# Eight tiles of probabilities, one mixing for each batch, and the FFN's low halves on VectorE, in a new order of operations

## The chip, the core and the metric

The kernel runs on one core of a Trainium2 chip. The metric is the device time of one execution in microseconds, the median of several runs. The engines are TensorE (PE), VectorE (DVE), ScalarE (ACT) and GpSimd (POOL); SP only issues DMAs. Each takes its instructions in the order of its own queue and waits at semaphores.

## The reference

64 batches of 128 tokens with 256 features pass through four residual blocks, each on the layer norm of x:

```
x = x + attention0(norm(x), ctx, mask)      # 16 heads of 16, biases, mask int32
x = x + ffn0(norm(x))                       # ternary W1, W2: relu(x W1' + b1) W2 + b2
x = x + attention1(norm(x), ctx, valid_len) # 16 heads of 16, no biases
x = x + ffn1(norm(x))                       # base + adapter of one of 8 experts
```

In an attention, scores are softmax(q k^T / 4) over 128 keys, and the output is that times v, times w_o. In ffn0, h = relu(...) has 1024 features. In ffn1 each batch takes the expert whose reconstruction relu(x Wd1 + bd1) Wd2 + bd2 is nearest to x, summed over the batch, and adds relu(x Wa_down + ba_down) Wa_up + ba_up of that expert.

## The kernel before

A pass handles a pair of batches (PB = 2, T = 256 tokens); there are NP = 32 pairs. The whole is a software pipeline written out by hand in slots. Each engine has one loop over the slots t, and `for p in at(t, 48)` runs an operation for the pair p whose slot 48 is t. BODY = 16 slots start a new pair, so operations of up to six pairs stand interleaved on each engine. The order within a slot and the slot numbers fix each queue's order. Waits are on counting semaphores: `signal.done(engine, p, n)` makes an engine wait for the n-th event of pair p.

Attention of layer l, for a pair: 8 steps j, each with four heads of one batch. `scores(l, p, j)` writes 128x512 scores into the one bank S. `maximum` on VectorE takes the row maxima from it. After four steps `split_max` splits the 16 maxima of a batch into fp16 halves and transposes them, and `maxima` on SP moves them into rows of qs by four DMAs. `scores_t` then computes the transposed scores less the maxima in the bank X, `exps` on ScalarE writes their exponentials into the tile pT, and for layer 0 `apply_mask` on GpSimd multiplies them by the mask. pT has 4 buffers of 128x512. `mix(l, p, u)` multiplies two buffers by the values in 8 matmuls (16 instructions, as each fp32 matmul is two) of 128 rows and 32 columns, which write the four column strips of the bank V; two mixings fill V for one batch. `turn_out` on VectorE transposes V, `scale_out` divides by the sums and transposes again into attT, and `output` multiplies by w_o. `add_att` adds to x.

q and k are kept as two fp16 halves: `high` on ScalarE copies the projection's bank as fp16, `low` on VectorE subtracts that. `spill` writes both to DRAM and `stack` reads them back with heads rearranged into qs and ks; both are issued by SP.

The FFN of layer 0: `ffn_up(p, j)`, four of them, write 128x512 into a bank. `relus` on ScalarE writes relu into work[j % 2] in fp32, `h_highs` on ScalarE rounds that to fp16 (hhl, part 0), and `h_lows` on GpSimd subtracts the rounded from the exact value (hhl, part 1). `ffn_down` for each of the two batches multiplies both parts by w2q.

ffn1: `hidden` and `reconstruct` (four, two experts each; 64-row matmuls), `differences` on VectorE, `squares` on ScalarE, `losses`, `choose`, a `gather` of the adapter by SP, `down` and `up`.

Layer norms: `statistics` on VectorE, `rstd_of` and `normalise` on GpSimd, `turn` on TensorE. `mask_parts`, `mask_bias` and `add_bias` are GpSimd's as well. `rstd_of(0, p)` also waits for `any_of` (VectorE), which reduces the mask to a column.

The other results of TensorE share five PSUM banks, D0 to D4; the table BANKS says which. A matmul that writes a bank waits for the consumer of the bank's last content.

Of the kernel before, what the change touches and what calls it, by code (L numbers as in the profile page):

```python
# [33 lines left out]
UNITS = 2 * PB  # L34
# [13 lines left out]
def pair16(value):  # L48
# [17 lines left out]
    ("cnt", "rec5", "v1", "hd0", "q0"),  # L66
    ("v0", "q1", "T2", "F1_1", "T0", "hd1", "T3"),
    ("O0", "F1_2", "rec1", "loss", "rec7", "up"),
    ("O1", "k0", "rec6", "rec3", "F2", "down", "rec0"),
    ("rec2", "F1_0", "T1", "k1", "F1_3", "rec4"),  # L70
# [27 lines left out]
def build(nc, x, lens, mask, mask_t, wq0, bq0, wk0, bk0, wv0, bv0, wo0, bo0, w1t, b1, w2t, b2,  # L98
          wq1, wk1, wv1, wo1, w_base, wd1, bd1, wd2, bd2, adapters, ctx_in, out):
    with ExitStack() as ctx:  # L100
# [76 lines left out]
        pT = sb("pT", [P, 4, 512], F32)  # L177
# [41 lines left out]
        mix_ready = [signal(f"mix_ready{l}", UNITS) for l in range(2)]  # L219
# [101 lines left out]
        def _(sp):  # L321
# [84 lines left out]
            for t in range(FIRST, END):  # L406
                for p in at(t, 48):
                    maxima(1, p, 1)
                for p in at(t, -14):
                    load(p)  # L410
                for p in at(t, 34):
                    stack(1, 1, p)
                    spill(1, 0, p)
                for p in at(t, 4):
                    maxima(0, p, 0)
                for p in at(t, 36):
                    stack(1, 0, p)
                for p in at(t, 71):
                    gather(p)
                for p in at(t, -7):  # L420
                    spill(0, 1, p)
                for p in at(t, 10):
                    maxima(0, p, 1)
                for p in at(t, -6):
                    stack(0, 1, p)
                for p in at(t, -5):
                    spill(0, 0, p)
                for p in at(t, 44):
                    maxima(1, p, 0)
                for p in at(t, -4):  # L430
                    stack(0, 0, p)
                for p in at(t, 76):
                    store(p)
                for p in at(t, 29):
                    spill(1, 1, p)
# [9 lines left out]
        def _(pool):  # L445
# [73 lines left out]
            def apply_mask(p, j):  # L519
                exp_done[0].done(pool, p, j)  # L520
                keep_ready.done(pool, p)
                blk = pT[:, j % 4].rearrange("p (a t) -> p a t", a=4)
# [3 lines left out]
            def h_lows(p, j):  # L526
                h_high.done(pool, p, j)
                nc.gpsimd.tensor_tensor(hhl[:, 1, 2 * j:2 * j + 2], work[:, j % 2], hhl[:, 0, 2 * j:2 * j + 2],  # L528
                                        ALU.subtract).then_inc(h_low.sem, 1)

            for t in range(FIRST, END):
                for p in at(t, 16):
                    normalise(1, p, 0)
                for p in at(t, 19):
                    normalise(1, p, 1)
                for p in at(t, -11):
                    mask_parts(p)
                    rstd_of(0, p)
                for p in at(t, -10):
                    normalise(0, p, 0)  # L540
                    normalise(0, p, 1)
                for p in at(t, 6):
                    apply_mask(p, 0)
                for p in at(t, 7):
                    apply_mask(p, 1)
                for p in at(t, 23):
                    h_lows(p, 0)
                for p in at(t, -8):
                    mask_bias(p)
                for p in at(t, 8):  # L550
                    apply_mask(p, 2)
                for p in at(t, 24):
                    h_lows(p, 1)
                for p in at(t, 9):
                    apply_mask(p, 3)
                for p in at(t, 26):
                    add_bias(1, p)
                for p in at(t, -6):
                    add_bias(0, p)
                for p in at(t, 26):  # L560
                    h_lows(p, 2)
                    h_lows(p, 3)
                for p in at(t, 10):
                    apply_mask(p, 4)
                for p in at(t, 58):
                    rstd_of(3, p)
                for p in at(t, 59):
                    normalise(3, p, 0)
                    normalise(3, p, 1)
                for p in at(t, 11):  # L570
                    apply_mask(p, 5)
                for p in at(t, 12):
                    apply_mask(p, 6)
                for p in at(t, 13):
# [15 lines left out]
        def _(act):  # L590
# [32 lines left out]
            def exps(l, p, j):  # L623
                st_ready[l].done(act, p, j)
                if j >= 4:
                    mix_ready[l].done(act, p, (j - 4) // 2)
                elif l:
                    mix_ready[0].done(act, min(p + 2, NP - 1), 2 + j // 2)
                    mix_ready[1].done(act, p - 1, 2 + j // 2)
                else:  # L630
                    mix_ready[1].done(act, p - 3, 2 + j // 2)
                    mix_ready[0].done(act, p - 1, 2 + j // 2)
                nc.scalar.activation(pT[:, j % 4], X[:], ACT.Exp, scale=SCALE).then_inc(exp_done[l].sem, 1)  # L633
# [54 lines left out]
            for t in range(FIRST, END):  # L688
                for p in at(t, 48):
                    exps(1, p, 2)  # L690
                for p in at(t, 64):
                    squares(p, 1)
                for p in at(t, 49):
                    exps(1, p, 3)
                for p in at(t, 66):
                    squares(p, 2)
                for p in at(t, 50):
                    exps(1, p, 4)
                for p in at(t, 34):
                    copy_xT(2, p)  # L700
                for p in at(t, 67):
                    squares(p, 3)
                for p in at(t, 51):
                    exps(1, p, 5)
                for p in at(t, 35):
                    high(1, 0, p)
                for p in at(t, 67):
                    squares(p, 4)
                for p in at(t, 52):
                    exps(1, p, 6)  # L710
                for p in at(t, 20):
                    copy_xT(1, p)
                for p in at(t, 68):
                    squares(p, 5)
# [3 lines left out]
                for p in at(t, 69):  # L718
                    squares(p, 7)
                for p in at(t, 6):  # L720
# [3 lines left out]
                for p in at(t, -9):  # L724
                    high(0, 1, p)
# [742 lines left out]
```

## Time and profile before

| | |
|---|---|
| median of 3 runs | 1717.36 us |
| lowest and highest | 1717.09 and 1728.58 us |
| profiled execution, own time | 1727.22 us |
| its span in the trace | 1725.2 us |
| PE busy | 1584.5 us (92%) |
| DVE busy | 1316.8 us (76%) |
| ACT busy | 891.8 us (52%) |
| POOL busy | 1104.2 us (64%) |

The span runs from the first to the last instruction of one profiled execution. Busy shares are means over the span, which has a ramp at either end in which few pairs are in flight. A busy TensorE is not one at its peak, since ends of matmuls are modelled; the starts are measured, so costs are read as the distance between starts.

### The profile page before, as it was taken

Reading aid. Unit: us, or ns where it says so; the run is one execution under the profiler, and the core shown is the slowest. Engines: PE = TensorE matmul, PEld = TensorE weight load, DVE = VectorE, ACT = ScalarE, POOL = GpSimd, SP = SyncE. Lnnn points to the kernel's source line nnn. Section 1 sums busy time; section 2 is a strip of 40 time slices with the busy share of each in tenths; the row PEclk is TensorE's granted clock in tenths of the full one; section 3 lists DMA queues with packets and bytes.
Section 4 is the critical chain, followed back from the end, with each engine's and each line's share of the span. In section 5 each row is a group of like instructions: output and inputs, shape, how many; then the busy total and the mean of one; then the engine's idle time right before and its main releaser. Section 6 shows DMA issues by size and latency. Waiting matters only on the chain.

```text
span 1725.2 us, 44058 instructions
## 1 busy us (share of the span) xinstructions
PE 1584.5 (92%) x15136; PEld 1279.1 (74%) x15136; DVE 1316.8 (76%) x5086; ACT 891.8 (52%) x2465; POOL 1104.2 (64%) x1198
## 2 busy tenths in 40 slices
PE   2578999999999999999999999999999999999776
PEld 1356777778878887778887877788788877877554
DVE  6446788888887888888887888888788888886542
ACT  0134455655555556555555556555555565555432
POOL 4467776666676776666667766666677766655200
PEclk9789999999999999999999999999999999999976
DMA  7445555555555454555555545555555555552300
GB/s 187 81 74 92 87 88 92 96 103 97 97 95 108 83 96 96 103 97 94 97 103 94 94 90 98 101 95 99 97 106 82 97 97 102 97 77 54 57 18 26
DMA packets 286213, 157.24 MB, mean 91 GB/s; under 512 B 38820, under 2 KB 281640, under 8 KB 285992
## 3 DMA queue, kind: packets, MB, share of 16 engines
q1 hardware_dynamic: 285992, 154.44, 49.6%
q8 instruction: 121, 1.98, 0.6%
q14 instruction: 100, 0.82, 0.2%
HBM read 111.36 MB, written 41.96 MB: 89 GB/s over the span
## 4 chain that ended last, share of the span: by engine, by line
PE 47%; DVE 38%; issue 7%; DMA 3%; POOL 2%; ACT 1%; SPq 1%; DVEq 0%; ACTq 0%; POOLq 0%
DVE dump L863 11%; PE psD L1239 7%; PE psD L1228 7%; DVE dif L929 6%; PE psD L1207 4%; PE psD L1153 4%; PE psD L1273 4%; PE psS L1168 3%; PE psD L1142 3%; PE psV L1195 3%; PE psX L1180 3%; DVE atok L894 3%; PE psD L1249 3%; DVE otok L886 2%; DVE m L872 2%
## 5 line engine op out<-in xcount | busy, mean ns | idle before, releaser
L633 ACT ACTIVATE pT<-psX 128x512 f32<-128x512 f32 x512 | 305.9, 597 | 351.7 <-PE psX L1180 351.6
L523 POOL TENSOR_TENSOR pT<-pT,keep 128x512 f32<-128x512 f32 x256 | 323.1, 1268 | 108.2 <-ACT pT L633 105.6
L508 POOL TENSOR_SCALAR xn<-xr,mv,rstd 128x256 f32<-128x256 f32 x256 | 311.5, 1224 | 13.7
L855 DVE TENSOR_REDUCE mx<-psS 128x4 f32<-128x512 f32 x256 | 175.7, 686 | 170.8 <-PE psS L1168 168.4
L482 POOL TENSOR_SCALAR veps<-mv 128x2 f32<-128x2 f32 x128 | 29.5, 230 | 392.3 <-DVE mv L808 389.6
L929 DVE SCALAR_TENSOR_TENSOR dif<-psD,bd2s,xT 128x256 f32<-128x256 f32 x512 | 216.8, 472 | 63.6 <-PE psD L1249 63.5
L863 DVE CUSTOM_DVE_ANT_0 dump<-psS,bias 128x128 bf16<-128x128 f32 x1024 | 232.5, 282 | 30.8 <-PE psS L1168 30.7
L1168 PE MATMUL psS<-ks,qs 65*128 65x128 f16 x2048 | 202.6, 221 | 49.2 <-DVE mx L863 22.6
L677 ACT ACTIVATE dif<-dif 128x256 f32<-128x256 f32 x512 | 207.4, 412 | 25.8 <-DVE dif L929 24.7
L1180 PE MATMUL psX<-qs,ks 67*128 67x128 f16 x2048 | 200.4, 220 | 15.5 <-ACT pT L633 8.7
L1168 PEld LDWEIGHTS psS<-ks,qs 65*128 65x128 f16 x2048 | 141.6, 98 | 97.8 <-issue 34.0
L1180 PEld LDWEIGHTS psX<-qs,ks 67*128 67x128 f16 x2048 | 141.6, 98 | 55.6 <-issue 18.6
L1195 PE MATMUL psV<-pT,v 128*32 128x128 f32 x4096 | 165.9, 280 | 8.0 <-POOL pT L523 4.3
L528 POOL TENSOR_TENSOR hhl<-work,hhl 128x512 f16<-128x512 f32 x128 | 151.5, 1193 | 11.9 <-ACT hhl L663 11.9
L1207 PE MATMUL psD<-wo,attT 128*128 128x256 f32 x512 | 132.1, 403 | 19.3 <-DVE attT L898 19.2
L1249 PE MATMUL psD<-hd,wd2s 64*128 64x256 f32 x1024 | 146.3, 405 | 2.0 <-DVE dif L929 2.0
L1195 PEld LDWEIGHTS psV<-pT,v 128*32 128x32 f32 x4096 | 96.8, 109 | 61.4 <-issue 39.3
L1220 PE MATMUL psD<-xs,w1q 128*128 128x256 f16 x1024 | 134.0, 274 | 1.4 <-DVE xs L911 0.8
L1142 PE MATMUL psD<-xT,wq 128*128 128x256 f32 x512 | 132.0, 394 | 1.5 <-DVE keep L822 1.5
L1153 PE MATMUL psD<-wv,ctxT 128*128 128x256 f32 x512 | 130.5, 399 | 0.0
L606 ACT ACTIVATE xT<-psD 128x512 f32<-128x512 f32 x96 | 57.1, 595 | 137.4 <-PE psD L1113 137.4
L1239 PE MATMUL psD<-xT,wd1s 128*128 128x256 f32 x512 | 126.0, 390 | 0.7 <-ACT xT L606 0.7
(103 smaller groups left out, 3125.3 us busy)
## 6 DMA issues: line engine op xcount, KB each, us to landing
scr<-packed SPq DMA_DIRECT2D x128, 256.0 KB, 2.3
ks<-scr SPq DMA_DIRECT2D x256, 128.0 KB, 4.5
qs<-scr SPq DMA_DIRECT2D x256, 128.0 KB, 4.4
adapter<-in_adapters SPq DMA_DIRECT2D x64, 192.5 KB, 2.5
xr<-in_x SPq DMA_DIRECT2D x32, 256.0 KB, 2.8
ctxT<-in_ctx SPq DMA_DIRECT2D x32, 256.0 KB, 2.8
qs<-mrows SPq DMA_DIRECT2D x512, 2.0 KB
out_y<-xr SPq DMA_DIRECT2D x32, 256.0 KB, 4.9
```

What stands on the lines that cost most here:

```text
L508: nc.gpsimd.tensor_scalar(xn[:, XN[s], b], xr[:, p % NX, b], mv[:, s, b, 0:1], rstd[:, s, b:b + 1], ALU.subtract, ALU.mult).then_inc(norme ...
L523: nc.gpsimd.tensor_tensor(blk, blk, keep[:, p % 2, j // 4].unsqueeze(1).to_broadcast([P, 4, P]), ALU.mult).then_inc(masked.sem, 1)
L633: nc.scalar.activation(pT[:, j % 4], X[:], ACT.Exp, scale=SCALE).then_inc(exp_done[l].sem, 1)
L677: nc.scalar.activation(blk, blk, ACT.Square, accum_out=acc[:, e, b:b + 1]).then_inc(squared.sem, 1)
L863: ins = nc.vector.tensor_tensor_reduce(out=dump[:, a], in0=S[:, a * P:a * P + P], in1=bias0[:, p % 2, b], scale=1.0, scalar=-3e38, op0=ALU ...
L929: nc.vector.scalar_tensor_tensor(out=dif[:, e % 4, k], in0=bank[f"rec{e}"][:, k * T:k * T + T], scalar=bd2s[:, e, k:k + 1], in1=xT3[:, p % ...
L1153: ins = nc.tensor.matmul(dst[:, b * D:b * D + D], ctxT[:, p % NC, k * T + b * P:k * T + b * P + P], wv[l][:, k], start=(k == 0), stop=(k = ...
L1168: ins = nc.tensor.matmul(S[:, a * P:a * P + P], qs[0:MASK_ROW + 1, r, h, t0:t0 + P], ks[0:MASK_ROW + 1, r, h, t0:t0 + P], start=True, stop ...
L1180: ins = nc.tensor.matmul(X[:, a * P:a * P + P], ks[0:ROWS, r, h, t0:t0 + P], qs[0:ROWS, r, h, t0:t0 + P], start=True, stop=True)
L1195: ins = nc.tensor.matmul(V[32 * a:32 * a + 32, (2 * half + s) * P:(2 * half + s) * P + P], v2[l][:, b, half * UH + 2 * a + s], pT[:, (2 * ...
L1207: ins = nc.tensor.matmul(dst[:, b * D:b * D + D], attT[:, l, b, k], wo[l][:, k], start=(k == 0), stop=(k == KD - 1))
L1239: ins = nc.tensor.matmul(dst[:, m * T:m * T + T], wd1s[:, k, e0:e0 + 2].rearrange("p e r -> p (e r)"), xT3[:, p % 2, k], start=(k == 0), s ...
```

## The change

pT gets 8 buffers, one for each step j. A mixing is now one of 16 matmuls (32 instructions) for a batch, `mix(l, p, b)`: it waits for the fourth exponential (or mask) of its batch. `exps` waits for the mixing that last read its buffer, of the other layer. `h_lows` moves from GpSimd to VectorE (the same function, there on nc.gpsimd). BANKS is dealt anew, and nearly every operation of every engine gets another slot or another place in its slot. Nothing of what is computed changes.

```
-        pT = sb("pT", [P, 4, 512], F32)
+        pT = sb("pT", [P, QUADS, 512], F32)
...
             def exps(l, p, j):
                 st_ready[l].done(act, p, j)
-                if j >= 4:
-                    mix_ready[l].done(act, p, (j - 4) // 2)
-                elif l:
-                    mix_ready[0].done(act, min(p + 2, NP - 1), 2 + j // 2)
-                    mix_ready[1].done(act, p - 1, 2 + j // 2)
+                if l:
+                    mix_ready[0].done(act, min(p + 2, NP - 1), j // 4)
                 else:
-                    mix_ready[1].done(act, p - 3, 2 + j // 2)
-                    mix_ready[0].done(act, p - 1, 2 + j // 2)
-                nc.scalar.activation(pT[:, j % 4], X[:], ACT.Exp, scale=SCALE)
+                    mix_ready[1].done(act, p - 3, j // 4)
+                nc.scalar.activation(pT[:, j], X[:], ACT.Exp, scale=SCALE)
...
+            def h_lows(p, j):
+                h_high.done(dve, p, j)
+                nc.vector.tensor_tensor(hhl[:, 1, 2 * j:2 * j + 2], work[:, j % 2], hhl[:, 0, 2 * j:2 * j + 2],
+                                        ALU.subtract).then_inc(h_low.sem, 1)
...
-            def mix(l, p, u):
-                b, half = u // 2, u % 2
-                if half == 0:
-                    claim("V", turned[l], p, b)
-                if u == 0:
+            def mix(l, p, b):
+                claim("V", turned[l], p, b)
+                if b == 0:
...
-                (exp_done[1] if l else masked).done(pe, p, 2 * u + 1)
-                for s in range(2):
+                (exp_done[1] if l else masked).done(pe, p, 4 * b + 3)
+                for n in range(4):
                     for a in range(4):
-                        ins = nc.tensor.matmul(V[32 * a:32 * a + 32, (2 * half + s) * P:(2 * half + s) * P + P],
-                                               v2[l][:, b, half * UH + 2 * a + s], pT[:, (2 * u + s) % 4, a * P:a * P + P],
+                        ins = nc.tensor.matmul(V[32 * a:32 * a + 32, n * P:n * P + P],
+                                               v2[l][:, b, n // 2 * UH + 2 * a + n % 2], pT[:, 4 * b + n, a * P:a * P + P],
```

The new order, by slot modulo 16 (`op@slot`), where the prediction speaks of it:

```
TensorE  0 values(1)@48, scores(0,0)@0, scores_t(1,2), reconstruct 1
         6 scores_t(0,0), scores(0,6), ffn_up 0@22, losses@70, mix(1,1)@54
         8 count@-8, keys(1)@24, scores_t(0,2), scores(1,0)@40, ffn_up 2@24
         9 ffn_up 3@25, scores_t(0,3), scores(1,1), turn(0)@-7, output(1)@57
        10 scores(1,2), down@74, scores_t(0,4), queries(0)@-6, mix(0,0)@10
        11 scores(1,3), scores_t(0,5), up@75
        12 ffn_down 0, scores_t(0,6), turn(3), scores(1,4)
        13 ffn_down 1, scores(1,5), scores_t(0,7), hidden 0
        14 scores_t(1,0), scores(1,6)
        15 hidden 1, scores(1,7), mix(0,1)@15, reconstruct 0@63, scores_t(1,1)
VectorE  0 differences 0, 1, scale_out(0,1)@16, maximum(0,0)@0, differences 2
         6 any_of@-10 (was -12), maximum(0,6), low(0,1), choose, values0, scale_out(1,0)
         7 maximum(0,7), h_lows 0@23
         8 split_max(0,1), maximum(1,0), turn_out(1,1), scale_out(1,1)@56
         9 maximum(1,1), h_lows 1, add_att(1)
        10 any_rows, maximum(1,2), h_lows 2, statistics(3)
        11 h_lows 3, low(0,0), maximum(1,3)
        12 turn_out(0,0), low(1,1)@28 (was @24, slot 8), add_up, split_max(1,0)@44, maximum(1,4)
        15 maximum(1,7), turn_out(0,1)@15, split_max(1,1)@47
GpSimd   4 mask_parts@-12, rstd_of(0)@-12
         5 mask_bias, apply_mask 0, normalise(0,0)
         6 apply_mask 1, normalise(0,1)   7 add_bias(0), apply_mask 2   8 apply_mask 3
SP      10 spill(0,0)@-6, maxima(1,0)@42 (was @44)   11 spill(1,1)@27, stack(0,0)@-5
        12 store, maxima(1,1)@44
```

Before, the four mixings of a pair and layer stood in slots 0, 2, 4, 6 (layer 1) and 9, 11, 13, 15 (layer 0), reconstruct 0 before mix(0,3), and differences 0 and turn_out(0,1) at the end of slot 15.

## Rows read from the trace of the kernel before

**Rows 1.** Stretches: busy us (x instructions) of each engine, TensorE's clock, DMA share, GB/s.
```profile
903.00:923.30 20.30, 19.41 (x199) 15.53 (x195) 19.92 (x93) 15.03 (x44) 15.87 (x19) 1.00 0.39 80
...
923.30:946.10 22.80, 22.67 (x206) 19.02 (x207) 14.85 (x38) 8.78 (x21) 18.36 (x19) 1.00 0.55 85
```

**Rows 2.** The chain of waits, in order of time: start us, us, what.
```profile
897.40 0.29 DVE dump L863
...
923.43 1.97 PE psD L1207 x8
```

**Rows 3.** TensorE in order of time: start, us, line, tiles, shapes, count, [idle before].
```profile
916.00 0.40 PE L1168 MATMUL psS<-ks,qs 65*128 65x128 f16 x4 [0.40 <-DVE mx L863]
...
972.38 1.97 PE L1207 MATMUL psD<-wo,attT 128*128 128x256 f32 x8 [0.55 <-DVE attT L898]
...
976.64 1.05 PE L1264 MATMUL psD<-xT,adapter 128*128 128x128 f32 x8
...
977.62 0.65 PE L1195 MATMUL psV<-pT,v 128*32 128x128 f32 x16
...
981.31 0.39 PE L1168 MATMUL psS<-ks,qs 65*128 65x128 f16 x4
...
985.93 0.39 PE L1180 MATMUL psX<-qs,ks 67*128 67x128 f16 x4
986.25 0.64 PE L1195 MATMUL psV<-pT,v 128*32 128x128 f32 x16
...
991.39 1.13 PE L1249 MATMUL psD<-hd,wd2s 64*128 64x256 f32 x8
992.45 0.65 PE L1195 MATMUL psV<-pT,v 128*32 128x128 f32 x16
993.03 1.99 PE L1153 MATMUL psD<-wv,ctxT 128*128 128x256 f32 x8
```

**Rows 4.** VectorE in order of time, same columns.
```profile
905.55 1.66 DVE L929 SCALAR_TENSOR_TENSOR dif<-psD,bd2s,xT 128x256 f32<-128x256 f32 x4
...
907.67 0.65 DVE L837 TENSOR_TENSOR packed<-psD,packed 128x512 f16<-128x512 f32 x1
...
913.27 0.75 DVE L845 TENSOR_TENSOR v<-psD,bvb 128x256 f32<-128x256 f32 x2
...
921.11 0.68 DVE L837 TENSOR_TENSOR packed<-psD,packed 128x512 f16<-128x512 f32 x1
...
921.99 0.82 DVE L894 TENSOR_TENSOR atok<-otok,rden 128x256 f32<-128x256 f32 x1
...
944.42 0.77 DVE L886 STREAM_TRANSPOSE otok<-psV 128x256 f32<-128x256 f32 x2
```

**Rows 5.** VectorE and GpSimd in order of time, around two forms of contact.
```profile
905.37 2.43 POOL L508 TENSOR_SCALAR xn<-xr,mv,rstd 128x256 f32<-128x256 f32 x2
...
907.32 0.18 DVE L872 SCALAR_TENSOR_TENSOR m<-mx,m 128x16 f16<-128x16 f32 x1
...
910.72 0.41 DVE L814 TENSOR_REDUCE allc<-mqf 128x2 f32<-128x256 f32 x1
...
911.88 2.43 POOL L508 TENSOR_SCALAR xn<-xr,mv,rstd 128x256 f32<-128x256 f32 x2
...
918.40 1.16 POOL L528 TENSOR_TENSOR hhl<-work,hhl 128x512 f16<-128x512 f32 x1
...
918.51 1.08 DVE L872 SCALAR_TENSOR_TENSOR m<-mx,m 128x16 f16<-128x16 f32 x1
...
919.66 1.52 POOL L476 TENSOR_SCALAR bias<-mqf,allc 128x128 f32<-128x128 f32 x2
...
921.26 1.27 POOL L523 TENSOR_TENSOR pT<-pT,keep 128x512 f32<-128x512 f32 x1
```

**Rows 6.** SP's queue in order of time, and DMA issues of 900 to 949 (us to landing).
```profile
921.10 2.69 SPq L377 DMA_DIRECT2D qs<-mrows  x4
...
qs<-scr SPq DMA_DIRECT2D x8, 128.0 KB, 4.4
```

More of the change, by code:

```diff
@@ L433, in _ @@
                     store(p)
-                for p in at(t, 29):
-                    spill(1, 1, p)
+                for p in at(t, 44):
+                    maxima(1, p, 1)
                 if LATE_SLOT <= t < LATE_SLOT + len(LATE):
@@ L521, in apply_mask @@
                 keep_ready.done(pool, p)
-                blk = pT[:, j % 4].rearrange("p (a t) -> p a t", a=4)
+                blk = pT[:, j].rearrange("p (a t) -> p a t", a=4)
                 nc.gpsimd.tensor_tensor(blk, blk, keep[:, p % 2, j // 4].unsqueeze(1).to_broadcast([P, 4, P]),
                                         ALU.mult).then_inc(masked.sem, 1)
[L526 to L529, printed above, removed]
             for t in range(FIRST, END):
@@ L737, in _ @@
                     h_highs(p, 1)
+                for p in at(t, 9):
+                    exps(0, p, 3)
                 for p in at(t, -7):
@@ L741, in _ @@
                     h_highs(p, 2)
-                for p in at(t, 9):
-                    exps(0, p, 3)
                 for p in at(t, 26):
@@ L751, in _ @@
                     a_relus(p)
+                for p in at(t, 27):
+                    high(1, 1, p)
                 for p in at(t, -5):
@@ L973, in _ @@
                 for p in at(t, 64):
+                    differences(p, 0)
                     differences(p, 1)
+                for p in at(t, 16):
+                    scale_out(0, p, 1)
                 for p in at(t, 0):
                     maximum(0, p, 0)
-                for p in at(t, 16):
-                    scale_out(0, p, 1)
-                for p in at(t, 65):
+                for p in at(t, 64):
                     differences(p, 2)
@@ L990, in _ @@
                     statistics(1, p)
-                for p in at(t, 50):
+                for p in at(t, 67):
+                    differences(p, 4)
+                for p in at(t, 51):
                     turn_out(1, p, 0)
@@ L995, in _ @@
                 for p in at(t, 67):
-                    differences(p, 4)
                     differences(p, 5)
-                for p in at(t, 4):
+                for p in at(t, 3):
                     split_max(0, p, 0)
@@ L1327, in _ @@
                     scores_t(1, p, 7)
-                for p in at(t, -11):
-                    count(p)
                 for p in at(t, 5):
@@ L1345, in _ @@
                     scores(0, p, 7)
+                for p in at(t, 23):
+                    ffn_up(p, 1)
+                for p in at(t, -8):
+                    count(p)
                 for p in at(t, 24):
-                    ffn_up(p, 1)
                     keys(1, p)
@@ L1401, in _ @@
                     scores_t(1, p, 0)
-                for p in at(t, 47):
-                    scores(1, p, 7)
+                    scores(1, p, 6)
                 for p in at(t, 63):
```

292 lines of the change are left out of this document (141 added, 151 removed).

## The prediction

> **What bounds the kernel now.** I read the stretches first. In the middle of the run TensorE is granted its full clock (1.00, that is 2.4 GHz) and is busy 19.4 of 20.3 us and 22.7 of 22.8 us [rows 1]. It looks like a kernel bound by TensorE, but the same rows show VectorE busy 19.9 of 20.3 us in the first stretch and 14.9 of 22.8 us in the second. So I read the chain of waits next. It has two legs: it runs on VectorE from the first maximum of layer 0 (897.40) to the last transpose before output(1), and output(1) on TensorE starts when that lands (923.43) [rows 2]. From there it runs on TensorE alone to the next pair's first maximum. Output(1) starts again at 972.38 [rows 3], so a pair costs 48.95 us: 26.0 on VectorE, 22.9 on TensorE, 31 times over. The TensorE timeline shows what the VectorE leg costs TensorE: 0.55 us idle before output(1) and 0.40 before a scores block [rows 3]. Measured from start to start these are about 0.7 and 0.57 us. TensorE's blocks alone fill some 47.7 us of the 48.95.
>
> So two sums must be made: what TensorE's own work becomes, and what the loop through both engines becomes. The larger one is the period.
>
> **TensorE's own work.** A mixing of 16 instructions takes 0.58 us (992.45 to 993.03) [rows 3]. Eight full-array fp32 instructions of 128 columns (down) take 0.98 us including 0.09 before the mixing behind them, thus 0.11 each [rows 3]. Four column strips run side by side, so 0.58 is 4 x 0.11 plus 0.14 for leaving the mode. Entering it costs 0.09: scores before a mixing hold TensorE 0.32 us (985.93 to 986.25) where 0.23 is usual. A mixing of 32 is then 8 x 0.11 + 0.14 = 1.01 us, for 1.15 before. Four of these a pair save 0.56. The new order has 6 entries into a tiled mode instead of 8 (mixings stand next to reconstruct or losses), 0.19 more. Fewer fp32 blocks stand behind an f16 block, some 0.1 to 0.2. TensorE's own work falls from 47.7 to 46.8 us. The lower end is that 32 instructions run at the pace of the down block throughout: 46.8. The other end is that 64 instructions in a row are issued no faster than before: 47.3.
>
> **VectorE's leg.** VectorE gets four subtractions of 128x512. The nearest row is the low half of a key, 0.68 us from PSUM, 0.60 from start to start [rows 4]. Sources in SBUF may be anything from 0.55 to 0.68; I take 0.60. Only h_lows 0 stands in the leg that bounds; 1 to 3 stand behind output(1), where VectorE was idle 8 us a pair [rows 1]. In exchange low(1,1) leaves the leg (-0.60). At the front, turn_out(0,1) (944.42, 0.7 from start to start), a split_max and two differences (2.12 together, 905.55 to 907.67) [rows 4] now stand ahead of maximum(0,0). Before, they ran beside values(1). The leg now starts when mixing (0,1) is done, not at the first maximum. Of the old 26.0 us, 1.3 were blocked time (below). So the new leg unblocked is 26.0 - 1.3 + 2.8 + 0.6 - 0.6 = 27.5 us.
>
> **TensorE's leg of the loop** is from output(1) to the end of mixing (0,1). Before, output(1) to the last mixing's start took 20.07 (972.38 to 992.45) [rows 3]. Out of it go two mixings (1.15), reconstruct 0 (1.06, 991.39 to 992.45), which now follows, one scores block with it (0.23) and one entry (0.09). In comes one mixing of 1.01. That is 18.55; plus 1.01 for mixing (0,1) itself and 0.2 until VectorE sees it: 19.75. The loop is 27.5 + 19.75 = 47.25 us before any blocking, already above TensorE's 46.8.
>
> **What VectorE waits for on GpSimd.** The same 16-element instruction (L872) takes 0.18 us while GpSimd normalises, a tensor_scalar (907.32 in 905.37 to 907.80), and 1.08 us while it runs a tensor_tensor (918.51, until 919.56) [rows 5]. The multiply of scale_out(1,1) took 0.82 for 0.42 behind a mask multiply that began at 921.26 [rows 4, 5]. That is the 1.3 us. The multiply ends 0.28 after GpSimd's operation; it starts 0.14 before the end of it. So I take it that VectorE operations with two SBUF sources wait for a running tensor_tensor of GpSimd. h_lows is one. The change removes four tensor_tensor from GpSimd, but GpSimd stays busy without a gap from mask 0 to mask 3: GpSimd now stands in rstd_of(0) until VectorE's any_of, which moved two slots later, and then has a backlog.
>
> Both queues start from any_of, so their phase can be worked out. GpSimd: 0.8 us of small operations until it starts its next large one (from 910.72 + 0.41 to 911.88) [rows 5]; then mask_bias, 1.6 (919.66 to 921.26); then mask 0, normalise, mask 1, normalise and add_bias, each 1.22 from start to start, as the two normalises of 2.43 [rows 5]. So mask 1 runs from 4.8 to 6.1 us after any_of, and mask 2 starts at 8.5. VectorE: before, the eleven operations from values0 to the multiply of scale_out(1,1) took 8.72 (913.27 to 921.99) [rows 4]. The new order has the same ones between any_of and that multiply, with h_lows 0 for low(1,1), so 7.73 unblocked. The multiply of scale_out(1,0) meets mask 0's end (0.2). h_lows 0 comes at 5.2, in mask 1: it waits 0.8. The multiply of scale_out(1,1) then comes at 8.7, 0.2 to 0.3 after mask 2 began: it waits 0.95. Together 1.95 us for 1.3 before. The loop is 49.2. The bounds are no blocking at all (47.25) and a full operation before each of five candidates, some 5 us (52).
>
> The page SBUF - State Buffer of the Trainium skill (Who interferes with whom) says that a VectorE instruction with two SBUF inputs contends with a GpSimd instruction that reads SBUF. It speaks against this change. The trace agrees for tensor_tensor (1.08 for 0.18 us), not for normalise, which reads SBUF too; the fourth rival is what the whole rule would give.
>
> **The other queues.** ScalarE keeps its work, in new slots with idle time before most of it. exps no longer wait for half mixings: nothing waited there that the chain shows, so zero. If ScalarE were late, mask 2 would be, and the block at 8.7 would go. The SP queue: maxima(1,0), whose row maxima are ready only two slots later, now holds spill(1,1) and stack(0,0) behind it; see the slow rival.
>
> **From period to time.** The ramps (223 us) keep their shape; TensorE's savings of 0.9 us a pair count there for some four pairs, -3 or -4 us. Likeliest: 31 x (49.2 - 48.95) = +8, less 4: +4. The profiled execution took 1727.2 us (span 1725.2) and would take about 1731. The median of the three runs is 1717.4, so I put 1720 there. Under 1% (17 us) I call no difference.
>
> **Rivals.**
> The phase falls well (faster): if VectorE is 0.3 us earlier, or mask 2 later, the multiply of scale_out(1,1) starts at once. The period is 48.2: -23 - 4, 1690. For it: the margin is 0.2 to 0.3 on a sum of twenty durations. Against: h_lows 0 is locked to mask 1's end, so what follows has a fixed phase. Chance 0.25.
> TensorE is all that counts (much faster): hardly any blocking, period 47.2: -54 - 4, 1660. This needs GpSimd idle where the profile shows backlog. Chance 0.09.
> SP's queue becomes late (slower): from the end of up, VectorE does add_up and split_max(1,0) (1.2), SP issues maxima (2.7), the spill (0.4) and four stacks (2.7 at most, like maxima), which land 4.4 later [rows 6]: 11.5 us. TensorE has 13.3 from up to the next scores(0,0) (981.31 to 993.03 and 1.8 for values, less 0.2). The reserve is 1.8 plus 0.5 that the first maximum waits anyway. From there on each us is a us a pair. Two blocks of 1.1 at split_max's two operations, or landings 2 us longer under the load of the other transfers, use it up. With those and a third block in the first leg the period is 50.2: +39 - 4, 1752. Chance 0.21.
> GpSimd's normalise blocks the subtraction as well (slower): then split_max(0,1) behind h_lows 0 waits for the rest of a normalise, 1.1, and the multiply before it for another 0.6. The period is 50.9: +60 - 4, 1773. The row at 907.32 is against it. Chance 0.03.
> The mixing of 32 takes twice the time of 16 (that part doing nothing): 0.28 on the loop, 1729, inside the likeliest case.
>
> **Chances.** Likeliest 0.42 (1703 to 1734), fast phase 0.25, floor 0.09, the two slow ones 0.24. Faster by over 1% 0.34, within 1% 0.41, slower 0.25. The range reaches to the fast phase and into the slow case: 1678 to 1754.
>
> **What would show it.** Mixing from first to next start 1.01 us; VectorE's share near 88 to 90%; GpSimd's share down by about 5 us a pair; h_lows on VectorE longer than 0.68 us in the profile for the first of four; output(1) still released by attT, with TensorE idle about 2 us there; the chain still VectorE then TensorE. I am wrong if output(1) is released without idle time, if the subtraction is blocked by nothing, or if scores(0,0) waits for qs<-scr.

## The result, and the profile after

The median went from 1718.43 to 1734.69 us (8 runs each, 1716.68 to 1728.58 and 1731.21 to 1741.07): a ratio of 1.0072, 95% interval 1.0050 to 1.0094. The ratio is not the quotient of those two medians (1.0095): the kernel before scatters by nearly as much as the change costs, five of its eight runs from 1716.68 to 1719.50 and three from 1724.63 to 1728.58, and its median on the chips of the experiments below is 1725 us. By the ratio the kernel is 0.7% slower, inside the range and within the 1% that I called no difference; with before at 1717.36, as in the prediction, that is 1729.7 us for 1720. The profiled execution took 1741.07 us, the slowest of its eight, 6.4 us over their median, and its span is 1739.1 us; before, 1727.22 and 1725.2. So differences between the two profiles, 13.8 us of span, are somewhat larger than those of typical runs. The page after, its busy time and its chain:

```profile
PE 1574.1 (91%) x15136; PEld 1286.0 (74%) x15136; DVE 1439.9 (83%) x5214; ACT 893.2 (51%) x2465; POOL 1020.0 (59%) x1070
...
PE 46%; DVE 35%; issue 12%; DMA 2%; POOL 2%; ACT 2%; SPq 1%; POOLq 0%; DVEq 0%; ACTq 0%
```

VectorE has 123 us more, GpSimd only 84 less: the four subtractions took 151.5 us there, but what it kept got longer, the 256 mask multiplies by 34 us and the 256 normalises by 18. The stretches that answer to [rows 1]:

```profile
908.00:930.40 22.40, 20.90 (x226) 17.07 (x225) 22.01 (x102) 16.10 (x49) 15.32 (x18) 1.00 0.65 113
930.40:953.60 23.20, 23.12 (x221) 19.36 (x222) 18.82 (x45) 8.63 (x19) 16.48 (x16) 1.00 0.55 82
```

TensorE's idle time in the first stretch grew from 0.9 to 1.5 us. Its timeline shows where, and answers to [rows 3]:

```profile
928.54 0.40 PE L1162 MATMUL psS<-ks,qs 65*128 65x128 f16 x4 [0.48 <-DVE mx L836]
...
930.48 1.99 PE L1199 MATMUL psD<-wo,attT 128*128 128x256 f32 x8 [1.10 <-DVE attT L879]
...
949.36 1.08 PE L1187 MATMUL psV<-pT,v 128*32 128x128 f32 x32
950.37 1.14 PE L1241 MATMUL psD<-hd,wd2s 64*128 64x256 f32 x8
...
954.36 1.14 PE L1241 MATMUL psD<-hd,wd2s 64*128 64x256 f32 x8 [0.30 <-ACT v L624]
...
979.70 1.99 PE L1199 MATMUL psD<-wo,attT 128*128 128x256 f32 x8 [1.10 <-DVE attT L879]
```

Output(1) is still released by the last transpose on VectorE, and waits longer than before (1.10 for 0.55 us). The next one starts 49.22 us later. A mixing takes 1.01 us (949.36 to 950.37). The chain that answers to [rows 2]:

```profile
951.83 1.80 PE psD L1147 x8
953.65 0.67 ACT v L624 x2
954.36 1.16 PE psD L1241 x8
955.58 0.36 issue
955.95 0.25 DVE dif L915
```

So the front of VectorE's leg isn't its own queue. It is values(1), ScalarE's copy of it out of bank D0, reconstruct 1, whose first half (rec2) goes into the same bank, and its differences.

VectorE and GpSimd around the contacts, in order of time, for [rows 4, 5]:

```profile
923.73 0.60 DVE L875 TENSOR_TENSOR atok<-otok,rden 128x256 f32<-128x256 f32 x1
...
925.55 1.66 DVE L897 TENSOR_TENSOR hhl<-work,hhl 128x512 f16<-128x512 f32 x1
927.13 0.16 DVE L851 TENSOR_SCALAR m<-mx 128x16 f16<-128x16 f32 x1
927.33 0.33 DVE L853 SCALAR_TENSOR_TENSOR m<-mx,m 128x16 f16<-128x16 f32 x1
...
929.49 0.45 DVE L875 TENSOR_TENSOR atok<-otok,rden 128x256 f32<-128x256 f32 x1
```

And GpSimd beside them:

```profile
925.39 1.27 POOL L523 TENSOR_TENSOR pT<-pT,keep 128x512 f32<-128x512 f32 x1
926.65 1.66 POOL L508 TENSOR_SCALAR xn<-xr,mv,rstd 128x256 f32<-128x256 f32 x1
928.39 1.27 POOL L515 TENSOR_TENSOR xr<-xr,bob 128x512 f32<-128x512 f32 x1
929.62 3.12 POOL L523 TENSOR_TENSOR pT<-pT,keep 128x512 f32<-128x512 f32 x2
```

h_lows 0 (925.55) waits for mask 1 and takes 1.66 us. While its second part runs, the normalise takes 1.66 instead of 1.22 us. That moves add_bias and mask 2, so the multiply of scale_out(1,1) at 929.49 meets only the last 0.17 us of add_bias, starts ahead of mask 2, and takes 0.45 us for 0.42: as good as not blocked.

**What the pairs add up to.** The starts of losses on TensorE, pair after pair, give 31 intervals. The first 26 are at full length, the last five are the drain. Before, the 26 are 48.93 to 49.02, sum 1272.6 us. After, 19 are 49.2 to 49.5 (mean 49.27) and 7 are 50.7 to 50.9 (mean 50.77), sum 1291.5. With the drain (205.0 for 205.9), the time ahead of the first start (225.7 for 229.6) and behind the last (16.9 for 17.2) the span is 13.8 us longer. In the long intervals output(1) itself is slow. Two stretches, ahead of such a one and in it:

```profile
1125.40:1127.70 2.30, 0.89 (x9) 0.66 (x9) 2.20 (x7) 2.02 (x4) 2.22 (x3) 1.00 0.02 2
1127.90:1131.20 3.30, 3.30 (x9) 2.40 (x9) 0.89 (x2) 0.84 (x2) 2.01 (x2) 0.50 0.78 111
```

The same output(1) in TensorE's timeline:

```profile
1127.65 3.66 PE L1199 MATMUL psD<-wo,attT 128*128 128x256 f32 x8 [1.09 <-DVE attT L879]
```

TensorE was busy 0.89 of 2.30 us, and then its granted clock is 0.50, that is 1.2 GHz. The eight matmuls take 3.66 us for 1.99. Each such fall costs its pair about 1.5 us. Between 200 and 1530 us there are 8 in the profiled execution after (7 in the 26 intervals, one in the drain) and none before; at the two ends of the run, where TensorE often stands idle, both have falls. So of the 18.9 us that the 26 intervals grew in this execution, 7 x 1.50 = 10.5 are the clock and 8.4 are the loop.

### The profile page after: what moved, and what is told of

Its sections match the earlier page's. It is cut to its first block, busy times and chain, and to the rows that moved or that the text cites. A ratio compares the mean times of both kernels' runs of the same rounds, so it can differ in the third digit from the quotient of the medians.

```text
span 1739.1 us, 43752 instructions
## 1 busy us (share of the span) xinstructions
PE 1574.1 (91%) x15136; PEld 1286.0 (74%) x15136; DVE 1439.9 (83%) x5214; ACT 893.2 (51%) x2465; POOL 1020.0 (59%) x1070
## 4 chain that ended last, share of the span: by engine, by line
PE 46%; DVE 35%; issue 12%; DMA 2%; POOL 2%; ACT 2%; SPq 1%; POOLq 0%; DVEq 0%; ACTq 0%
DVE dump L844 9%; PE psD L1231 6%; PE psD L1220 6%; DVE dif L915 5%; PE psD L1199 5%; PE psD L1241 4%; PE psD L1147 4%; PE psV L1187 4%; PE psD L1265 3%; PE psD L1136 3%; PE psS L1162 3%; DVE hhl L897 3%; PE psX L1174 3%; DVE otok L867 2%; DVE atok L875 2%
## 5 line engine op out<-in xcount | busy, mean ns | idle before, releaser
L523 POOL TENSOR_TENSOR pT<-pT,keep 128x512 f32<-128x512 f32 x256 | 357.3, 1401 | 134.4 <-ACT pT L616 131.9
L508 POOL TENSOR_SCALAR xn<-xr,mv,rstd 128x256 f32<-128x256 f32 x256 | 329.9, 1295 | 10.1
L482 POOL TENSOR_SCALAR veps<-mv 128x2 f32<-128x2 f32 x128 | 38.9, 304 | 406.2 <-DVE mv L789 403.7
L1199 PE MATMUL psD<-wo,attT 128*128 128x256 f32 x512 | 144.4, 431 | 35.6 <-DVE attT L879 35.6
L1187 PE MATMUL psV<-pT,v 128*32 128x128 f32 x4096 | 143.4, 282 | 5.7 <-POOL pT L523 5.7
L640 ACT ACTIVATE work<-psD,b1s 128x256 f32<-128x256 f32 x256 | 107.5, 471 | 78.8 <-issue 34.5
L1199 PEld LDWEIGHTS psD<-wo,attT 128*128 128x128 f32 x512 | 103.0, 211 | 57.3 <-DVE attT L879 39.0
L1124 PE MATMUL psD<-ctxT,wk 128*128 128x256 f32 x512 | 126.1, 390 | 14.0 <-DVE bqr L952 13.8
L1187 PEld LDWEIGHTS psV<-pT,v 128*32 128x32 f32 x4096 | 107.9, 112 | 30.1 <-issue 26.6
L897 DVE TENSOR_TENSOR hhl<-work,hhl 128x512 f16<-128x512 f32 x128 | 126.9, 992 | 3.7 <-ACT hhl L646 3.7
```

What stands on the lines that cost most here:

```text
L508: nc.gpsimd.tensor_scalar(xn[:, XN[s], b], xr[:, p % NX, b], mv[:, s, b, 0:1], rstd[:, s, b:b + 1], ALU.subtract, ALU.mult).then_inc(norme ...
L1187: ins = nc.tensor.matmul(V[32 * a:32 * a + 32, n * P:n * P + P], v2[l][:, b, n // 2 * UH + 2 * a + n % 2], pT[:, 4 * b + n, a * P:a * P + ...
L1199: ins = nc.tensor.matmul(dst[:, b * D:b * D + D], attT[:, l, b, k], wo[l][:, k], start=(k == 0), stop=(k == KD - 1))
```

## The experiments

Ratios are against the kernel before on the same chip: its median was 1725.58 us beside fill3 to swap_pool, 1724.93 beside no_mask to combo, and 1725.23 beside the last three. "Period" is the median of the first 27 intervals between starts of losses in the profiled execution. "Falls" are the stretches at 0.50 of TensorE's clock between 200 and 1530 us.

| kernel | median us | ratio, 95% interval | period us | falls |
|---|---|---|---|---|
| after | 1734.69 | 1.0072 (1.0050 to 1.0094) | 49.24 | 8 |
| fill3 | 1725.58 | 1.0008 (0.9990 to 1.0026) | 49.20 | 0 |
| late_lows | 1745.91 | 1.0119 (1.0082 to 1.0156) | 49.87 | 0 |
| bank_swap | 1733.09 | 1.0048 (1.0029 to 1.0067) | 49.07 | 4 |
| swap_pool | 1776.82 | 1.0296 (1.0258 to 1.0334) | 51.36 | 21 |
| no_mask | 1708.76 | 0.9911 (0.9895 to 0.9926) | 48.79 | 0 |
| lows_on_pool | 1894.86 | 1.0986 (1.0965 to 1.1007) | 54.42 | 27 |
| merge_alone | 1745.05 | 1.0116 (1.0101 to 1.0132) | 49.68 | 0 |
| combo | 1763.41 | 1.0220 (1.0204 to 1.0237) | 50.20 | 0 |
| lows_first | 1718.72 | 0.9968 (0.9956 to 0.9980) | 48.75 | 0 |
| lows_first_bank | 1713.20 | 0.9939 (0.9919 to 0.9959) | 48.67 | 0 |
| lows_first_bias | 1711.84 | 0.9929 (0.9910 to 0.9947) | 48.48 | 0 |

**fill3: TensorE kept busy ahead of output(1).** Three matmuls that are no work of the reference go into output(1)'s bank before its wait.

```
+                if l:
+                    for n in range(3):
+                        nc.tensor.matmul(dst[:, 0:D], ident[:], wb[:, 0], start=True, stop=True)
```

> The changed kernel with three filler fp32 matmuls of 128x256 (six instructions, 1.3 us at the full clock) issued by TensorE ahead of the wait in output(1), into the bank that output(1) then overwrites. They do no work of the reference. Theory (the half-clock windows follow from TensorE's idle 1.1 us before output(1)): no half clock in the steady stretch, the pairs of 50.8 us gone, period 49.2 in all, since the fillers only fill a wait; about 12 us less than the changed kernel, 1722. Rival (the half clock is the chip's answer to load, whatever the idle time): the pairs of 50.8 us stay or grow in number, 1735 or more. Rival (TensorE's own work sets the time): plus 1.3 us a pair, 1775.

TensorE's timeline of fill3:

```profile
1067.45 1.46 PE L1197 MATMUL psD<-wb,ident 128*128 128x256 f32 x6
1068.75 1.96 PE L1203 MATMUL psD<-wo,attT 128*128 128x256 f32 x8
```

The fillers (L1197) stand where the idle time was. All falls are gone, the period is what it was, and 1.0072 becomes 1.0008. So the falls are caused by TensorE's idle time here, and they make up most of the loss in the ratio. What is left, 0.08%, isn't clear of the noise, although the period of 49.20 for 48.94 says that the loop is slower.

**late_lows: h_lows 0 out of the leg.** It goes behind scale_out(1,1), with four buffers of `work` for two so that relu 2 needn't wait for it.

```
-        work = sb("work", [P, 2, 2, T], F32)
+        work = sb("work", [P, 4, 2, T], F32)
...
-                for p in at(t, 23):
-                    h_lows(p, 0)
...
                 for p in at(t, 25):
+                    h_lows(p, 0)
                     h_lows(p, 1)
```

> The changed kernel with a work tile of four buffers in place of two, and h_lows 0 moved on VectorE from between maximum(0,7) and split_max(0,1) to behind scale_out(1,1). Theory (the loop runs through VectorE's queue from differences 2 to scale_out(1,1), and h_lows 0 holds 1.6 us of it, 0.7 of work and 1.0 of waiting for GpSimd): period 47.7 to 48.2, hardly any idle time before output(1), no half clock; 1685 to 1700. Rival (the wait only moves: the next VectorE operation with two SBUF sources meets the next tensor_tensor of GpSimd): period 48.6 to 49.2, 1710 to 1730. Rival (TensorE's order of work sets the period): no change, 1733.

VectorE's timeline of late_lows:

```profile
1032.47 1.02 DVE L847 TENSOR_SCALAR m<-mx 128x16 f16<-128x16 f32 x1
...
1035.55 0.74 DVE L871 TENSOR_TENSOR atok<-otok,rden 128x256 f32<-128x256 f32 x1
...
1037.28 2.37 DVE L893 TENSOR_TENSOR hhl<-work,hhl 128x512 f16<-128x512 f32 x2
...
1041.43 1.32 DVE L893 TENSOR_TENSOR hhl<-work,hhl 128x512 f16<-128x512 f32 x1
```

The wait moved and grew. Split_max's first operation, 0.13 us where it is free, now meets mask 1 (1.02), and the multiply meets add_bias (0.74). Behind output(1) the subtractions wait for masks too (1.75 for h_lows 1, 1.32 for h_lows 2), and the chain stays on VectorE until 1044.82, as up's bank waits for the low half of the queries. I had called the place behind output(1) free, as VectorE was idle there; with one subtraction more and 1.7 us of waiting in it (1.75 + 1.32 for twice 0.68) it isn't. The rival was right in kind, and its period of 48.6 to 49.2 too low.

**bank_swap: rec2, the first half of reconstruct 1, from bank D0 to D4.**

```
-    ("O1", "F1_0", "q0", "rec2", "v1", "rec5", "T1", "up"),
+    ("O1", "F1_0", "q0", "v1", "rec5", "T1", "up"),
...
-    ("T0", "rec6", "k0", "F1_2", "down", "F1_1", "hd0", "T3", "T2"),
+    ("T0", "rec2", "rec6", "k0", "F1_2", "down", "F1_1", "hd0", "T3", "T2"),
```

> The changed kernel with rec2 moved in the table of banks from D0, where it follows v1, to D4, where it follows hd0. Theory of the trace after the change (the chain passes through ScalarE's copy of v1, for which reconstruct 1 waits because of the shared bank): reconstruct 1 starts 0.3 to 0.5 us earlier and the period falls by 0.2 to 0.4, 1722 to 1729, if VectorE is ready for differences 2 by then. Rival, my prediction's own account (VectorE's queue with turn_out, split_max, two differences and scale_out is what holds the front): no change within 0.1 us a pair, 1733.

The chain of bank_swap, behind an output(1) at 1021.65:

```profile
1040.61 1.05 PE psV L1187 x32
1041.68 0.78 DVE otok L867 x2
...
1042.90 1.62 DVE dif L915 x4
...
1044.71 0.44 DVE atok L875
...
1046.50 0.40 PE psS L1162 x4
```

The period falls by 0.15 us, less than the 0.2 to 0.4 of the theory. The front of the leg was indeed the shared bank. Behind it stands what the prediction had: 20.0 us after output(1) mixing (0,1) is done, and VectorE's queue with turn_out, split_max, two differences and scale_out takes over. In the time the gain doesn't show: the median is 1733.09 us, and the interval of the ratio overlaps that of the changed kernel. The profiled execution was the fastest of the ten (1724.95 us at a mean granted clock of 0.965; the slowest took 1737.41 at 0.954), so its 4 falls are probably fewer than the usual run has.

**swap_pool: GpSimd's order turned.** Its second normalise goes ahead of mask 1.

```
-                for p in at(t, 6):
-                    apply_mask(p, 1)
                 for p in at(t, -10):
                     normalise(0, p, 1)
+                for p in at(t, 6):
+                    apply_mask(p, 1)
```

> The changed kernel with GpSimd's normalise(0,1) ahead of apply_mask 1, where it was behind it; the same operations. Theory (h_lows 0 waits 1.0 us because it comes while GpSimd runs the tensor_tensor of mask 1, and not while it normalises): h_lows 0 now falls at the end of the normalise or the start of the mask, the profile shows it at 0.7 or at up to 1.7 us by that phase, and the period changes by the difference of all VectorE's waits on GpSimd, 48.2 to 49.4. Rival (GpSimd's normalise blocks it as well): h_lows 0 stays above 1 us also in those cases in which it starts inside the normalise, period 49.2.

VectorE's timeline of swap_pool:

```profile
1044.99 0.95 DVE L897 TENSOR_TENSOR hhl<-work,hhl 128x512 f16<-128x512 f32 x1
...
1046.13 1.20 DVE L853 SCALAR_TENSOR_TENSOR m<-mx,m 128x16 f16<-128x16 f32 x1
...
1049.15 0.88 DVE L875 TENSOR_TENSOR atok<-otok,rden 128x256 f32<-128x256 f32 x1
```

h_lows 0 no longer waits a whole mask (0.95), but split_max (1.20 for 0.18) and the multiply (0.88) do. The loop is 49.8 where the clock holds and 51.3 where it falls, and it falls in nearly every pair. Neither theory had that size. GpSimd does the same work in both orders, so here the order alone costs 0.6 us a pair (49.8 for 49.2), and the falls the rest.

**no_mask: no mask multiplies.** The attention of layer 0 isn't masked in this kernel; VectorE's wait for the masks, ahead of writing the next ones, goes too.

```
             def apply_mask(p, j):
-                exp_done[0].done(pool, p, j)
-                keep_ready.done(pool, p)
...
+                return
...
-                (exp_done[1] if l else masked).done(pe, p, 4 * b + 3)
+                exp_done[l].done(pe, p, 4 * b + 3)
```

> The changed kernel without GpSimd's eight mask multiplies of a pair (apply_mask does nothing, the mixing of layer 0 waits for the exponentials alone): the attention of layer 0 is not masked. It takes away nearly all tensor_tensor work that GpSimd runs beside VectorE's stretch from any_of to scale_out(1,1). Theory (waiting for GpSimd's tensor_tensor costs the loop of both engines 1.2 to 1.5 us a pair, 1.0 of it at h_lows 0): h_lows 0.68 to 0.7 us in nearly all cases, period 47.6 to 48.2, no half clock, 1680 to 1700. Rival (the blocked time is hidden, TensorE's order or the banks set the period): h_lows short, but the period 49.0 to 49.2, 1725 to 1735.

VectorE's timeline of no_mask, then GpSimd's:

```profile
1004.72 1.77 DVE L892 TENSOR_TENSOR hhl<-work,hhl 128x512 f16<-128x512 f32 x1
```
```profile
1004.68 1.27 POOL L515 TENSOR_TENSOR xr<-xr,bob 128x512 f32<-128x512 f32 x1
```

Even without the masks the subtraction is blocked, now by add_bias. That it would take 0.68 us was a miss. The loop still gains 0.4 us, as the multiply and split_max go free. That is less than half of what the theory had (47.6 to 48.2). It also bears on the clock: output(1) still waits 1.07 us here, and no fall follows.

**lows_on_pool: h_lows back on GpSimd, all else as after.** h_lows 0 goes before mask 2, h_lows 1 before mask 4, the other two behind it.

```
                 for p in at(t, -9):
                     add_bias(0, p)
+                for p in at(t, 23):
+                    h_lows(p, 0)
                 for p in at(t, 7):
                     apply_mask(p, 2)
...
+                for p in at(t, 25):
+                    h_lows(p, 1)
                 for p in at(t, 9):
                     apply_mask(p, 4)
+                for p in at(t, 26):
+                    h_lows(p, 2)
+                    h_lows(p, 3)
```

> The changed kernel with h_lows back on GpSimd (0 ahead of mask 2, 1 ahead of mask 4, 2 and 3 behind it), all else in its new place. Theory (h_lows 0 on VectorE costs the loop 1.6 us; on GpSimd it leaves behind only the waits of others for a fifth tensor_tensor in that stretch): period 47.8 to 48.6, 1685 to 1715. Rival (GpSimd, which stands until any_of and then has a backlog, becomes the late one: masks, then normalise(0,1) and turn(0)): period 49.5 or more, with TensorE waiting for GpSimd ahead of turn(0) or a mixing; 1745 or more.

GpSimd's timeline of lows_on_pool, then TensorE's:

```profile
1009.66 1.21 POOL L508 TENSOR_SCALAR xn<-xr,mv,rstd 128x256 f32<-128x256 f32 x1
1010.96 1.26 POOL L515 TENSOR_TENSOR xr<-xr,bob 128x512 f32<-128x512 f32 x1
1012.18 1.33 POOL L528 TENSOR_TENSOR hhl<-work,hhl 128x512 f16<-128x512 f32 x1
```
```profile
1014.49 1.11 PE L1106 MATMUL psD<-ident,xn 128*128 128x128 f32 x4 [3.19 <-ACT work L652]
```

GpSimd works without a gap from any_of on, the subtraction ends at 1013.5, and relu 2 on ScalarE and TensorE behind it wait for that (3.19 us idle). The rival was right in kind and the price, 5 us a pair, far above either number. In the new order the subtractions can't stay on GpSimd at these places. Other places there weren't tried.

**merge_alone: the kernel before, with eight tiles and one mixing for a batch only.** The mixings of a batch stand where its second half stood, in slots 50 and 54, 11 and 15.

```
-                for p in at(t, 48):
-                    mix(1, p, 0)
...
                 for p in at(t, 50):
                     scores_t(1, p, 4)
-                    mix(1, p, 1)
+                    mix(1, p, 0)
```

> The kernel before with the eight tiles and the mixing for a batch alone: the four mixings of a pair stand where the second half stood (slots 2, 6, 11 and 15), nothing else moves. Theory (the loop of both engines sets the period, so only what lies between output(1) and the next first maximum counts: three half mixings of 0.58 with three entries of 0.09 become two whole of 1.01 with two entries): plus 0.2 us a pair there, period 48.9 to 49.2, the same time as before within 0.5%. Rival (TensorE's total work sets the time, and it falls by 0.6 to 0.8 us a pair): period 48.2 to 48.3, 1.3% faster than before.

The chain of merge_alone, in order of time:

```profile
1022.42 0.60 ACT pT L631
1023.01 0.49 ACT xs L606
1023.50 1.19 ACT dif L675 x6
...
1032.08 1.03 DVE m L870
...
1036.95 1.10 PE psD L1203 x4
```

The period rises by 0.74 us. The chain (above) still ends in VectorE's leg and output(1), and now comes to it through ScalarE. TensorE's busy time hardly moves (1582.3 us for 1584.5) while the span grows by 18 us, so the 0.6 to 0.8 us a pair that the rival expected it to save don't show in this order, and it isn't TensorE's work that makes the kernel slower. My own theory had +0.2 and missed the size; which of the later mixings costs the 0.7 wasn't taken apart. At these places the longer mixing is worth nothing alone.

**combo: bank_swap, two fillers, and add_bias(0) in slot 15.**

```
-                for p in at(t, -9):
-                    add_bias(0, p)
...
+                for p in at(t, -1):
+                    add_bias(0, p)
                 for p in at(t, 15):
                     rstd_of(1, p)
```

> The changed kernel with rec2 in D4, two filler matmuls ahead of the wait in output(1) (0.9 us, no work of the reference), and GpSimd's add_bias(0) moved from between normalise(0,1) and mask 2 to slot 15, where GpSimd stands waiting for statistics(1). Theory (waits for GpSimd's tensor_tensor in the stretch, the bank of v1 and the half clock are each worth 0.1 to 0.5%): period 48.6 to 49.0, no half clock, 1700 to 1718, at or under the kernel before. Rival (the block moves to the next tensor_tensor, as it did when h_lows 0 was moved): period 49.0 to 49.3, 1718 to 1728.

VectorE's timeline of combo, then GpSimd's:

```profile
1014.68 1.22 DVE L852 TENSOR_SCALAR m<-mx 128x16 f16<-128x16 f32 x1
```
```profile
1014.60 1.27 POOL L516 TENSOR_TENSOR xr<-xr,bob 128x512 f32<-128x512 f32 x1
```

The moved add_bias met split_max(1,1) at the front of the leg, in a place where GpSimd had been free, and blocks it by 1.1 us in every pair. In 11 of the 26 full intervals the multiply of scale_out(1,1) is blocked as well, by 1.14 us, and they take 51.2 to 51.5 us where most others take 50.1. No falls, yet 2.2% slower, beyond both theory and rival.

**lows_first: h_lows 0 ahead of maximum(0,7).** One swap on VectorE, so that the subtraction starts before mask 1 does.

```
+                for p in at(t, 23):
+                    h_lows(p, 0)
                 for p in at(t, 7):
                     maximum(0, p, 7)
-                for p in at(t, 23):
-                    h_lows(p, 0)
```

> The changed kernel with one swap on VectorE: h_lows 0 ahead of maximum(0,7) in place of behind it; the same operations. Theory (what h_lows 0 costs the loop beyond its 0.6 us is the phase: behind maximum(0,7) it meets mask 1, which began 0.15 us earlier; ahead of it, it meets the normalise before that mask, a tensor_scalar, and starts at once): h_lows 0 at 0.7 us, the period 0.3 to 0.9 lower, 48.3 to 48.9, fewer half clocks, 1700 to 1722. Rival (the blocked time moves to scale_out(1,1) or split_max(0,1), as when h_lows 0 was moved to the end): h_lows 0 at 0.7 but the period 49.0 to 49.5, 1730 or more.

VectorE's timeline of lows_first, then GpSimd's:

```profile
1010.04 0.65 DVE L897 TENSOR_TENSOR hhl<-work,hhl 128x512 f16<-128x512 f32 x1
1011.57 0.42 DVE L851 TENSOR_SCALAR m<-mx 128x16 f16<-128x16 f32 x1
...
1014.05 0.75 DVE L875 TENSOR_TENSOR atok<-otok,rden 128x256 f32<-128x256 f32 x1
```
```profile
1009.34 1.39 POOL L508 TENSOR_SCALAR xn<-xr,mv,rstd 128x256 f32<-128x256 f32 x1
1010.70 1.26 POOL L523 TENSOR_TENSOR pT<-pT,keep 128x512 f32<-128x512 f32 x1
```

The subtraction lies inside a normalise and takes 0.65 us for 1.66. Of that 1.0, split_max gives back 0.13 (0.42 + 0.20 for 0.16 + 0.33) and the multiply 0.30 (0.75 for 0.45). The loop is 48.75, below before's 48.94, and the falls are gone: the theory, in period and time.

**lows_first_bank and lows_first_bias.** The first adds bank_swap. The second adds to that both add_bias between mask_parts and rstd_of(0), where GpSimd stood waiting for any_of.

```
                 for p in at(t, -12):
                     mask_parts(p)
+                for p in at(t, 4):
+                    add_bias(0, p)
+                for p in at(t, 20):
+                    add_bias(1, p)
+                for p in at(t, -12):
                     rstd_of(0, p)
```

> As lows_first, and rec2 in D4 as in bank_swap. Theory (both add up, since they lie at different places of the same loop): 0.15 us a pair under lows_first, no half clock, 0.3% under it, 1695 to 1717. Rival (one of the two is hidden once the other is gone): the same as lows_first within 0.05 us a pair.

> As lows_first_bank, and GpSimd's two add_bias between mask_parts and rstd_of(0), where GpSimd otherwise stands waiting for any_of and VectorE has no operation with two SBUF sources. Theory (each tensor_tensor of GpSimd that leaves the stretches of split_max, scale_out and h_lows takes a possible wait with it): 0.1 to 0.6 us a pair under lows_first_bank, 1680 to 1710, faster than the kernel before. Rival (masks then run back to back and meet scale_out(1,1), which now just slips in ahead of mask 2): 0.3 to 1.2 us a pair more than lows_first_bank, 1720 or more.

Both beat before and after: 0.9939 and 0.9929. Their intervals overlap, so they can't be ranked. The bank is worth 0.08 us a pair here, half of the 0.15 expected and close to the rival's 0.05. In the last, the multiply takes 0.64 us and the period is 48.48, 0.2 lower as expected; its time of 1711.84 us is just above the 1710 of the theory. So the change as a whole pays once one subtraction stands elsewhere: 0.6 to 0.7% under the kernel before.

## Why the prediction came out as it did

**Two legs, output(1) released by attT.** Right. The leg's front was wrong in kind: I had VectorE's queue from the end of mixing (0,1) on, and the trace has bank D0 and ScalarE's copy ahead of the differences. bank_swap prices that at 0.15 us and shows the queue that I had right behind it. Of the 49.22 us, the chain has 25.1 from output(1) to the end of reconstruct 1 (930.48 to 955.58) and 24.1 on VectorE, where I had 19.75 and 29.45.

**TensorE's own work.** A mixing of 32 takes 1.01 us as worked out. The 0.9 us that TensorE saves a pair can be seen where no falls lengthen its matmuls: lows_first, with the same work on TensorE, has it busy for 1559.0 us, for 1584.5 before, 0.8 a pair. That its sum doesn't bound was right: lows_first gains its 0.48 us a pair by a swap on VectorE alone. TensorE's leg, from output(1) to the end of mixing (0,1) plus 0.2, took 20.16 us (930.48 to 950.44 in the chain) for 19.75. I didn't take that 0.4 apart.

**What VectorE waits for on GpSimd.** The mechanism held: mask 1 began 5.0 us after any_of ended (920.42), for 4.8, and h_lows 0 was blocked by it, 0.98 for 0.8. The multiply of scale_out(1,0) was blocked by 0.17 for 0.2. The third block, 0.95 on the multiply of scale_out(1,1), didn't come. I let mask 2 start 8.5 us after any_of, and it started at 9.2, mostly as the subtraction itself stretches the normalise (1.66 for 1.22). So 1.15 blocked, for 1.95.

**The period.** 49.2 predicted, 49.22 from output(1) to output(1). It is right by luck as well, by terms that cancel: less blocking (-0.8) against TensorE's leg (+0.4), split_max's second operation (0.33 for 0.18, +0.15), and what is left for the front of the leg and the rest of the 27.5 (+0.27). VectorE is 90% busy over the two stretches, as said, though 83% over the span. GpSimd's 5 us a pair became 2.6 (84 of 32 pairs), since its other operations were lengthened. The idle time before output(1) is 1.1 us, where I had said 2.

**From period to time: the term that was missing.** I took 31 intervals; only 26 are at full length, so the loop's term is 8.4, by chance what I had put (31 x 0.25 = +8), as the plain intervals are a little above 49.2. The 223 us that I gave the ramps don't come out either: 31 intervals of 48.95 leave 208 of the span. The sum doesn't use them. The ramps gave -3.9 ahead, -0.9 in the drain and -0.3 behind, for -4. The term that I hadn't is the clock: seven falls in the 26 intervals, +10.5 us in the profiled execution. [rows 1] showed a full clock, and I took it to stay so although I lengthened the idle time myself. By my sum the ratio was 1720.0 / 1717.36 = 1.0015; it is 1.0072, and without the falls (fill3) 1.0008.

**The rivals.** SP's queue: the two blocks that this rival needed did come, in part: split_max(1,0) takes 0.53 and 1.19 us (940.91 and 941.48) beside a mask and add_bias. But the reserve held: between 230 and 1517 us, scores blocks wait for their DMA three times, 0.8 us in all. The phase that falls well came in one place (scale_out(1,1)) and its gain went elsewhere. Normalise blocks too: lows_first refutes it, its subtraction starting 0.70 us into a normalise and taking 0.65. The page SBUF - State Buffer of the Trainium skill (Who interferes with whom) counts any GpSimd instruction that reads SBUF; here GpSimd's tensor_tensor blocks and its tensor_scalar doesn't, though it is slowed itself (1.22 to 1.39 there). TensorE is all that counts: refuted by lows_first, where TensorE's work is the same and the period isn't.

## What to carry to other kernels

A VectorE operation like those blocked here (the subtraction, split_max's two, the multiply) costs its own time plus what is left of a GpSimd tensor_tensor that has begun: when one is moved, write down which GpSimd operation runs beside each VectorE operation of the chain behind it, and put the long one inside a tensor_scalar or a wait of GpSimd's. A leg that makes TensorE idle has a second price, the clock, so count the idle time of the whole neighbourhood and not only the wait itself. Try an order with one swap at a time: single moves here gave between -0.5 (lows_first) and +2.1 us a pair (swap_pool).

## What the runs showed of the hardware that was not expected

**Falls of the clock without a long pause.** What TensorE did just ahead of output(1), idle us before the scores block behind ffn_up and before output(1), at 2.4 GHz:

| kernel | idle before scores | idle before output(1) | falls |
|---|---|---|---|
| after | 0.48 | 1.10 | 8 |
| swap_pool | 0.70 | 1.52 | 21 |
| bank_swap | 0.47 | 1.10 | 4 |
| fill3 | 0.47 | 0 | 0 |
| late_lows | 0 | 1.30 | 0 |
| no_mask | 0.31 | 1.07 | 0 |
| lows_first | 0 | 0.71 | 0 |

It isn't the wait before output(1) alone: late_lows waits longer there than after and never falls. Nor is it enough that two waits stand close together: no_mask has 0.31 and 1.07 and never falls. The kernels of this table that fall have the longest two together. One long wait seems to do it too: lows_on_pool, with 3.19 us ahead of turn(0), falls 27 times. And the same pair of waits falls in some pairs only; what decides between them stays open.

**Contact costs both engines.** A mask multiply takes 1401 ns in the mean for 1268 before, a normalise 1295 for 1224; of the 151.5 us of subtractions that left GpSimd, 53 came back as longer masks and normalises. That it is contact is shown for single ones, such as the normalise of 1.66 us above; no run takes the whole apart.

**How a blocked operation ends.** The blocked first part of split_max in combo starts at 1014.68 and ends at 1015.90, GpSimd's span at 1015.87. Even an operation that reads 128x16 waits to the end.
